# A window-attention block: ScalarE's exponential and its copy of the turned probabilities change places in each slot

## The reference

```python
h = layernorm(x, norm1_g, norm1_b)              # per token
hw = h in windows of 64 tokens                  # 1024 windows
q, k, v = split(hw @ qkv_w + qkv_b)             # 3 heads of 16
attn = softmax(q * SCALE @ k.T + bias[REL_IDX])
out = (attn @ v) @ proj_w + proj_b
x = x + out in image order
h2 = layernorm(x, norm2_g, norm2_b)
return x + gelu(h2 @ fc1_w + fc1_b) @ fc2_w + fc2_b
```

## Time and profile before

| | |
|---|---|
| median of 3 runs | 1110.33 us (1105.14 to 1111.57) |
| the profiled execution | 1109.31 us, of which its span 1107.5 us |
| granted TensorE clock, mean | 0.988 of full speed |
| PE busy | 1052.1 us, 95% of the span |
| PE weight loads busy | 924.5 us, 83% |
| VectorE busy | 800.1 us, 72% |
| GpSimd busy | 757.8 us, 68% |
| ScalarE busy | 710.7 us, 64% |
| exponentials L787 | 256, mean 525 ns, 134.3 us |
| copies of turned probabilities L768 | 256, mean 488 ns, 125.0 us |

### The profile page before, as it was taken

The page is one execution under the profiler, slowest core; times in us unless marked ns, Lnnn a source line. Parts: engine busy times, 40 slices in busy tenths (PEclk is TensorE's granted clock), DMA queues, the critical chain, the costliest instruction groups (busy, mean ns, idle before and its releaser), DMA issues.

```text
span 1107.5 us, 26440 instructions
## 1 busy us (share of the span) xinstructions
PE 1052.1 (95%) x7366; PEld 924.5 (83%) x7366; DVE 800.1 (72%) x2301; ACT 710.7 (64%) x1347; POOL 757.8 (68%) x1174
## 2 busy tenths in 40 slices
PE   2899999999999999999999999998899999999997
PEld 0688888888888888888888888887699999999997
DVE  4667767777777777677777777767477777777773
ACT  1556676666766667666666666665466766666674
POOL 5367765667655677656776667764578888888881
PEclk9989999999999999999999999999699999999999
DMA  1001110001110011100111001100011111111111
GB/s 43 27 16 36 38 36 32 28 32 41 35 35 28 28 43 34 36 28 28 43 35 37 28 28 39 35 25 15 15 29 43 43 43 43 43 43 43 40 40 48
DMA packets 24807, 38.25 MB, mean 35 GB/s; under 512 B 4119, under 2 KB 20698, under 8 KB 24794
## 3 DMA queue, kind: packets, MB, share of 16 engines
q1 hardware_dynamic: 24722, 37.90, 10.9%
q10 hardware_dynamic: 72, 0.20, 0.0%
HBM read 25.50 MB, written 12.58 MB: 34 GB/s over the span
## 4 chain that ended last, share of the span: by engine, by line
issue 34%; PE 32%; POOL 29%; DVE 2%; POOLq 1%; ACT 1%; DMA 1%; ACTq 0%; DVEq 0%
PE scores_ps L594 15%; POOL rstd L377 11%; POOL lowered L464 6%; PE x_ps L587 5%; PE x_ps L581 4%; POOL centred L373 4%; POOL normed L383 3%; PE x_ps L571 3%; PE scores_ps L539 1%; PE mixed_ps L554 1%; POOL small L365 1%; DMA x_in<-in_x 1%; POOL small L359 1%; POOL small L368 1%; POOL small L364 1%
## 5 line engine op out<-in xcount | busy, mean ns | idle before, releaser
L464 POOL TENSOR_TENSOR lowered<-biased,row_top 128x384 f32<-128x384 f32 x256 | 212.1, 829 | 264.1 <-DVE row_top L980 263.6
L787 ACT ACTIVATE probs<-lowered 128x384 f32<-128x384 f32 x256 | 134.3, 525 | 180.7 <-POOL lowered L464 179.8
L377 POOL TENSOR_TENSOR rstd<-small,minus_half 128x4 f32<-128x4 f32 (+1 forms) x160 | 242.9, 1530 | 0.0
L554 PEld LDWEIGHTS mixed_ps<-v_blocks,probs_t 128*128 128x128 f32 x1536 | 196.0, 193 | 44.7 <-ACT probs_t L768 24.4
L539 PE MATMUL scores_ps<-k_blocks,q_blocks 96*128 96x192 f32 x1024 | 225.9, 344 | 1.6 <-DVE q_blocks L968 1.6
L554 PE MATMUL mixed_ps<-v_blocks,probs_t 128*128 128x66 f32 x1536 | 209.4, 273 | 7.8 <-ACT probs_t L768 3.4
L976 DVE TENSOR_TENSOR biased<-scores_ps,pos 128x384 f32<-128x384 f32 x256 | 142.2, 555 | 83.1 <-PE scores_ps L539 79.1
L594 PEld LDWEIGHTS scores_ps<-wfc,hidden 128*128 128x128 f32 x1536 | 181.0, 192 | 6.2 <-issue 0.5
L594 PE MATMUL scores_ps<-wfc,hidden 128*128 128x96 f32 x1536 | 179.9, 274 | 0.3 <-ACT heads_t L803 0.3
L768 ACT ACTIVATE probs_t<-probs_t_ps 128x384 f32<-128x384 f32 x256 | 125.0, 488 | 82.3 <-PE probs_t_ps L546 80.4
L539 PEld LDWEIGHTS scores_ps<-k_blocks,q_blocks 96*128 96x128 f32 x1024 | 163.8, 193 | 4.3 <-DVE q_blocks L968 2.1
(11 more groups left out here) (100 smaller groups left out, 1615.1 us busy)
## 6 DMA issues: line engine op xcount, KB each, us to landing
x<-in_x SPq DMA_DIRECT2D x128, 96.0 KB
out<-x SPq DMA_DIRECT2D x128, 96.0 KB
x_in<-in_x SPq DMA_DIRECT2D x244, 48.0 KB
x_second<-in_x SPq DMA_DIRECT2D x8, 48.0 KB
x_in<-in_x ACTq DMA_DIRECT2D x4, 48.0 KB
pos_in<-in_L_conv_rel_bias_table SPq DMA_DIRECT2D x8, 10.6 KB
wproj<-in_L_conv_proj_w SPq DMA_DIRECT2D x6, 3.0 KB
wfc_in<-in_L_conv_fc_w SPq DMA_DIRECT2D x2, 36.0 KB
```

Source lines behind the costliest of these rows:

```text
L377: pool.tensor_tensor(rstd[:, groups], small[:, 7, groups], minus_half[:, groups], ALU.pow).then_inc(step, 1)
L464: pool.tensor_tensor(lowered[:, k % 2, :, :], biased[:, k % 2, :, :], broadcast(row_top[:, k % 2, :], 2, TOK), ALU.subtract).then_inc(lowe ...
L554: mm = pe.matmul(mixed_ps[:, at:at + MIX], probs_t[:, h, :], v_blocks[:, part, u, h, :], start=True, stop=True)
L787: act.activation(probs[:, k % 2, :, :, :].rearrange("p h a t -> p a h t"), lowered[:, k % 2, :, :].rearrange("p (a h) t -> p a h t", a=2), ...
```

## The change

In each slot ScalarE first waits for the turned probabilities of quad k - 2 and copies them, and then waits for the lowered scores of quad k - 1 and takes their exponential. Before, it was the other way round. The slot's other copies stay behind both. No other engine's program is touched, and neither is the epilogue.

```diff
                 for k in range(QUADS):
+                    if not (first and k < 2):
+
+                        wait(act, probs_turned, s0 + k - 1)
+                        probs_t_out()
                     if not (first and k == 0):
                         exp_of(s0 + k - 1, (k - 1) % QUADS)
-                    if not (first and k < 2):
-
-                        wait(act, probs_turned, s0 + k - 1)
-                        probs_t_out()
                     if k == 0:
                         wait(act, v_mm, 2 * n + 1)
                         v_out(0)
```

More of the change, by code:

```diff
@@ L808, in body @@
                 for k in range(QUADS):
-                    if not (first and k == 0):
-                        exp_of(s0 + k - 1, (k - 1) % QUADS)
                     if not (first and k < 2):
@@ L814, in body @@
                         probs_t_out()
+                    if not (first and k == 0):
+                        exp_of(s0 + k - 1, (k - 1) % QUADS)
                     if k == 0:
```

## The result

The changed kernel takes 1117.49 us (median of ten runs, 1111.58 to 1120.06), the kernel before 1110.36 us beside it. The ratio is 1.0056, with a 95% interval from 1.0035 to 1.0076: slower by 0.6%, about 6 us by the ratio and 7.1 between the medians, where 10.5 us had been forecast. Three executions at a far lower granted clock (1318.31 us at 0.752 in the run with all slots but slot 4, 1765.27 us at 0.556 there and once more in the run with the split token copies) are left out of all medians and ratios here.

What follows compares the result with a forecast made beforehand. TensorE was taken as the bound, its projection of q waiting for tokens_t in each batch. 30 x 0.43 = 12.9 us, less 1.5, less 0.9, gave +10.5 us: 1120.8 us, range 1110 to 1130.

Steps and rivals of the forecast that it cites:

- The projection of q, with no room at all: Slot 4's token copies end later, so slot 5's projection of q starts 0.43 us later each batch, 12.9 us in all.
- the two readings of an exponential's price: Start-to-start time of an exponential and the next copy: 0.41 in the epilogue, 0.55 at 302.55; the forecast took 0.43.
- the rival without overlap: The exponential inserted ahead of slot 4's token copies costs 0.55 us, not 0.43: 1124.4 us; chance 0.17.
- What can come back is between 0 and 0.1 us a batch; I take 0.05.: Slot 7's copy of the turned probabilities comes earlier, so its mixing can start sooner: 1.5 us back in all.
- The added time covers that lateness, 0.9 us.: Batches lengthened by a late load of x, on average 0.03 us, absorb that much of the added time.
- 30 batches.: Batches that pay the delay: 31 have the token copies, less the first, which is bound elsewhere.
- A wait of 0.31 us ... which covers it; without that cover it would cost 0.3 us a batch.: Slot 2's later k copies delay slot 3's turning of heads by 0.3 us, hidden by the wait for GpSimd's normalised tokens.
- The exponential's lateness "at nothing": Exponentials run later, by up to 2 us in slot 4, but readers come in the next slot; cost taken as nothing.
- The swallowed delay: TensorE's 0.31 us wait in slot 3 for GpSimd's normalised tokens absorbs the delay; 1110.3 us; chance 0.10.
- The faster rival: The copy of slot 7 or 0 is on the loop; moving it ahead saves up to 0.43 us a batch, 1097.4 us; chance 0.06.
- The clock: The new wait in each slot 5 lowers TensorE's granted clock: +2 to +4 us a batch, 1180 to 1240 us; chance 0.03.

Runs made afterwards that it cites:

- the run with all slots but slot 4: Against the kernel before, the copy of the turned probabilities goes ahead of the exponential in every slot except slot 4; 1107.97 us, ratio 0.9969.
- the run with the split token copies: Kernel before, but in slot 4 the first of two token copies stands ahead of the copy of the turned probabilities; 1106.06 us, ratio 0.9965.
- slot 4 alone: Against the kernel before, the copy of the turned probabilities goes ahead of the exponential in slot 4 only; 1119.56 us, ratio 1.009.
- the double push: Changed kernel plus a second exponential into a spare tile in slot 4, pushing the token copies twice; 1125.44 us in one run.
- the run with both gains: Kernel before, with slot 4's first token copy ahead of its copy of the turned probabilities, and the copy first in slot 7; 1104.95 us, ratio 0.9948.
- a push of twice the size: Kernel before, with the copy first in slot 2 alone and a second exponential there into a spare tile; 1110.81 us in one run.

## Why the prediction was right, and where its sizes were off

The direction, the mechanism and the place were right, and 1117.5 lies in the range; the size was 10.5 us and came out as 7.0. Of the 3.5 us between them 29 x 0.07 = 2.0 lie in what slot 7 gives back, 29 x 0.04 = 1.2 in the price of the exponential, and the rest in one batch too many. The wait for tokens_t is 0.58 us in each batch, as the prediction said it would be, and no wait of TensorE for an exponential appears. By its terms:

*"The projection of q, with no room at all."* Right: the delay of tokens_t passes to the batch in full, shown by slot 4 alone (23.60) and by the double push (0.42 more). It was taken as 0.43 us and measured 0.39: 23.60 - 23.23 is 0.37 on the means, and the end of the token copies moved by 0.39 (two starts of 0.39 and 0.41, and a pair of copies that takes 2.02 instead of 2.04). Of the two readings of an exponential's price, the epilogue's 0.41 was the right one; 0.55 appeared at no inserted exponential shown here, so the rival without overlap fell. It had more behind it than the prediction saw: besides 302.55 the kernel before has the distance of 0.55 in slot 7 too, from the exponential at 314.79 to the copy at 315.34, and no run shows why these two are longer. The overlap that the Trainium skill states ("ScalarE: Activation LUTs", section "What ACT_TABLE_LOAD costs"), with which an ACTIVATE of this size is an estimate of 413 ns, agrees with the 0.41 of the inserted exponentials, and not with these two places.

*"What can come back is between 0 and 0.1 us a batch; I take 0.05."* This is the term that was mis-sized, and its upper bound was too low as well. Slot 7 gives back 0.12 to 0.13 us: with the same order in slot 4, 23.60 with slot 7 unchanged became 23.47 in the changed kernel, and the copy first in slot 7 alone brought short batches of 23.05 where the earlier trace rows have 23.20. I had read only the 0.05 us between the copy's end and the mixing's start. The rest is in the mixing itself, 0.89 before and 0.81 after: with the copy in time its first weight load starts 0.08 us ahead of its matmuls, beside those of the projection. The list of waits hardly shows it (33 waits in the earlier trace rows, 28 in the changed kernel), since it counts only idle time, and the weight loads of the projection ran until 314.86 + 0.97 = 315.83. The same 0.08 us showed in the projection of q when its wait went (1.10 to 1.02). That the overlapped load is what makes a group shorter is read from these starts and durations and was not measured apart.

*"The added time covers that lateness, 0.9 us."* Right in kind: in the changed kernel the batches are even. That late loads make batches uneven is shown for the run with both gains, by loading x earlier; for the kernel before it is argued from there. 0.39 - 0.12 - 0.03 = 0.24 us a batch, which is the measured beat.

*"30 batches."* 29 is what the steady part has, from the third batch to the last.

*"A wait of 0.31 us ... which covers it; without that cover it would cost 0.3 us a batch."* The cover held, but was priced too narrowly: in slot 2 a push of twice the size is free. The wait for the second half of the normalised tokens stands behind the first, and the weight loads for it start 2.73 us behind the scores with and without the push.

*The exponential's lateness "at nothing".* With the copy first in all slots but slot 4 the kernel is faster than before, so no late exponential of those slots costs anything that shows. The list of waits of the changed kernel puts 4 of GpSimd's 224 subtractions down to an exponential, 5.9 us in all, but no batch of the chain is longer for it.

*The rivals.* The swallowed delay: wrong for slot 4, but it is what happens in slot 2. The Trainium skill ("Perfetto Trace Analysis", section "Identifying the Most-Contended Engine") has the engine with the highest occupancy treated first; what the prediction drew from it for this rival, that an order on a 67% busy ScalarE would not move the end, does not hold here: the same swap is a loss of 0.39 us in slot 4 and a gain of 0.12 in slot 7. The faster rival had the right slot, with little over a quarter of its price, and lost to slot 4. The clock stayed at 1.00.

## What to carry to other kernels

Judge a swap on an in-order engine by what stands behind the pair, slot by slot: work that can run while the queue would wait anyway belongs ahead of the wait, and a swap that is a gain over seven places together can lose in one where a copy behind it is already waited for. A short wait that repeats once per iteration (0.19 us for tokens_t here) is the place to look: there every delay was paid at its full length. It is no proof by itself, for the weight loads of a mixing wait 0.57 us for probs_t in every batch of both kernels (28 times, 16.1 us, in the changed one), and the matmuls behind them start without a wait. And a wait for something else just behind the delayed work makes the delay free, as in slot 2. When one arm of a loop gets shorter, look at once for the next one: here a good part of the gain went into a load that was queued behind others, until it was issued first.

## What the runs showed of the hardware that I had not expected

In two places a wait on TensorE cost more than its idle time. Where the copy that a group waited for came in time, the group was also shorter: six mixing matmuls 0.81 us against 0.89, two projection matmuls 1.02 against 1.10, in each case about the 0.08 us by which the wait alone had under-priced it.

A copy out of PSUM, an exponential from SBUF and another copy follow each other on ScalarE at 0.39 and 0.41 us, though the first two are recorded with about 0.5; in these places a row's duration overstates the price of one more instruction by about a quarter.
